# Sequence stage of a fused state-space and expert layer: chunk states in 32-row strips, scores in 32x64 tiles, and paced scatters

## The chip, the cores and the metric

One core of one Trainium2 chip runs the kernel. The metric is the device time in microseconds, as the median of several executions. Everything is float32, except 0/1 tables in bfloat16 for the routing. A float32 product shows as two matmul records and two weight loads in the trace, a float32 transpose and a bfloat16 product as one each.

## The reference

The input x has 2048 tokens of 128 values. The first part is a chunked state-space layer with 16 heads of 8 values, 16 states per head and chunks of 64 tokens:

```python
proj = x @ W_in.T                       # xp | z | B (16x16) | C (16x16) | dt_low (16)
dt = softplus(dt_low @ dt_W.T + dt_b);  dA = dt * -exp(A_log);  dAcs = cumsum(dA) in each chunk
scores = einsum('bcihn,bcjhn->bcijh', Cc, Bc) * exp(dAcs_i - dAcs_j) * causal * dtc
y_intra = einsum('bcijh,bcjhp->bcihp', scores, xc)
chunk_state = einsum('bckhn,bckhp->bchnp', Bc, (dtc * decay_to_end)[..., None] * xc)
h = chunk_decay * h + chunk_state       # one step for each of the chunks, in order
y_cross = einsum('bcthn,bchnp,bcth->bcthp', Cc, h_states, exp(dAcs))
y = (y_intra + y_cross) + xp * D_param
y = y / rms(y) * norm_w * silu(z);      out = y @ W_out.T
x = layernorm(x + out)
```

The second part sends each token to 4 of 16 experts, by the four largest of the logits `-|x - key_e|^2 + x @ rw.T + rb`, with a softmax over the four; an expert is 128 to 512, gelu, 512 to 128. The result is `layernorm(x + the weighted sum of four)`.

## The kernel before

**Stages.** The tokens are 16 tiles of 128 (two chunks each), two tiles to a pair, 8 pairs. A start-up loads the inputs and computes all step sizes and decays. A sequence loop of seven steps (s = 1 to 7) then runs the tiles 2s and 2s + 1 through projection, scores and states, and the older pairs through output, norm and routing. Then come the experts: 64 full and 8 mixed blocks of 128 rows, in four-deep rings, and a final sum and norm. Every engine has its own in-order list of work; semaphores alone tie them together. The order of each list is written out by hand: for TensorE at lines 705 to 729, DVE at 1234 to 1290, ACT at 1731 to 1747, GpSimd at 1868 to 1913. SyncE (SP) issues loads in the order of lines 407 to 420, and the experts' row loads from line 423 on.

**The sequence step on TensorE.** `project` (L530) makes x and B of one tile in rows of tokens, 384 columns. `project_cb` (L539) makes B and C turned, four 128-column products. `scores` (L553) multiplies B with a block-diagonal copy of C (`block_diag`, ACT, L1641, four copies a tile, each masked for one of four heads), in tiles of 64 rows by 64 columns of the array, 256 columns each, into banks 3 and 4. `states` (L563) makes the two chunk states as full 128x128 products, of which only the blocks on the diagonal are of use. DVE carries the state from chunk to chunk by a sum and a scale for each (L949, L958), and `y_cross` (L578) reads it. `y_intra` (L591) uses 16-column tiles; its result, turned, is copied by ACT (`yiT_copy`, L1653) and added to y by `y_back` (L601). `skip_products` (L616), `y_transpose` (L622), `out_product` (L630), `x2_transpose` (L636), `router` (L642) and `positions` (L651 to 655) belong to older pairs and write two banks by turns (`late`).

**DVE and ACT.** DVE masks the scores (`causal`, L965), scales x (`take_x`, L940), forms y (`y_scale`, `y_add`, L990, L998), gates it (`gated`, L1005), adds x (`residual`, L1013), normalizes (`normed`, L1038), and finds the four experts, the slots (`slots`) and the gates. ACT copies between PSUM and SBUF and takes exponentials and logarithms.

**Scatters.** When a pair's normed rows, ids, gates and slots are there, GpSimd sends them to the experts' row table in HBM with eight indirect DMAs (L1860), one for each tile and choice. SP loads the first expert's rows (L447) only when the 40 scatters of pairs 0 to 4 have landed (`EARLY` = 5) and the early table is made. The scatters of pairs 5 and 6 stand in GpSimd's list ahead of the experts' first store of results (L1881), those of pair 7 are mixed with stores 7 to 14.

## Time and profile before

| what | us |
|---|---|
| median of 3 runs | 314.29 |
| lowest and highest run | 314.27, 315.08 |
| span of the profiled execution | 314.5 |
| TensorE busy | 283.4 (90%) |
| DVE busy | 204.3 (65%) |
| ACT busy | 209.2 (67%) |
| GpSimd busy | 143.7 (46%) |

The profiled execution's own time is its span, 314.5 us, from the first to the last instruction on the core; no other time of it is given. The start-up takes up to about 29 us, the sequence loop and its tail up to about 126, the experts up to about 282, the rest is the final sum. In a timeline row stand the start, the time to the end of the last of the merged instructions, the engine, the line, the output and input, and the count; a matmul's end is modelled, so the distance to the next group's start is the better price.

### The profile page before, as it was taken

How to read it: one execution, taken by the hardware profiler on the slowest of the kernel's cores; microseconds unless marked ns; L12 is line 12 of the kernel's file. 1: busy time of each engine (PE TensorE's matmuls, PEld its weight loads, DVE VectorE, ACT ScalarE, POOL GpSimd, SP SyncE). 2: the span in 40 equal slices, each digit the busy share in tenths (PEclk: the TensorE clock that was granted, in tenths of full speed). 3: DMA queues.
4: the chain of work that ended last, by engine and by line, in shares of the span. 5: the costliest groups of instructions: out<-in, count | busy, mean ns of one | idle time of the engine just before them, and what ended most of it. 6: DMA issues, size and time to landing. Idle time of an engine off the chain costs nothing.

```text
span 314.5 us, 10587 instructions
## 1 busy us (share of the span) xinstructions
PE 283.4 (90%) x2948; PEld 250.6 (80%) x2949; DVE 204.3 (65%) x914; ACT 209.2 (67%) x725; POOL 143.7 (46%) x146
## 2 busy tenths in 40 slices
PE   2999899999999997899889899999999999997591
PEld 2986668687677775799779899999999999995480
DVE  2237768898888888866888566555655566641272
ACT  1475466575574743577667688888888889885064
POOL 1200000657456474777677775555555564424000
PEclk9979999999999999599999999999999999999697
DMA  6999920111111111342122232222222222100884
GB/s 212 300 336 374 415 95 2 40 39 57 38 58 48 39 58 47 87 103 78 48 83 90 80 92 72 65 81 71 67 69 67 70 68 60 42 12 6 305 273 92
DMA packets 25260, 33.30 MB, mean 106 GB/s; under 512 B 4299, under 2 KB 18020, under 8 KB 24832
## 3 DMA queue, kind: packets, MB, share of 16 engines
q1 hardware_dynamic: 20432, 23.30, 24.7%
q0 software_dynamic: 4352, 8.79, 7.9%
q10 hardware_dynamic: 432, 0.67, 0.7%
q8 instruction: 22, 0.36, 0.5%
q14 instruction: 22, 0.18, 0.2%
HBM read 21.76 MB, written 11.50 MB: 106 GB/s over the span
## 4 chain that ended last, share of the span: by engine, by line
PE 70%; DVE 11%; DMA 6%; issue 5%; ACT 5%; POOL 1%; DVEq 1%; POOLq 0%; ACTq 0%; SPq 0%
PE bank L774 16%; PE bank L752 15%; PE bank L747 4%; PE bank L539 4%; PE bank L553 4%; DMA yrows<-shared,idi 3%; PE bank L844 3%; PE bank L764 3%; PE bank L530 2%; PE bank L736 2%; PE bank L514 2%; PE bank L591 2%; DMA small<-in_small 2%; PE bank L601 2%; PE bank L563 2%
## 5 line engine op out<-in xcount | busy, mean ns | idle before, releaser
L1881 POOL DMA_INDIRECT yrows<-shared,idi x72 | 75.9, 1054 | 56.1 <-ACT shared L1790 32.6
L1860 POOL DMA_INDIRECT xrows<-rows_all,sli x64 | 62.4, 975 | 81.6 <-issue 63.4
L1769 ACT ACTIVATE shared<-bank,shared 128x128 f32<-128x128 f32 x256 | 73.2, 370 | 19.1 <-PE bank L752 19.1
L752 PE MATMUL bank<-shared 128*128 128x128 f32 x512 | 70.0, 281 | 2.5 <-issue 2.5
L774 PE MATMUL bank<-w2s,shared 128*128 x512 | 68.1, 276 | 0.8 <-DVE shared L1464 0.4
L752 PEld LDWEIGHTS bank<-shared 128*128 128x128 f32 x512 | 63.8, 196 | 3.9 <-issue 3.8
L774 PEld LDWEIGHTS bank<-w2s,shared 128*128 128x128 f32 x512 | 62.3, 192 | 1.4 <-issue 1.4
L1450 DVE COPY shared<-w1s 128x644 f32 x64 | 33.1, 517 | 28.5 <-issue 27.7
L1790 ACT ACTIVATE shared<-shared,idg 128x128 f32<-128x128 f32 x72 | 29.9, 418 | 7.1 <-DVE shared L1464 5.8
L1641 ACT ACTIVATE shared<-bank,small 128x256 f32<-128x256 f32 x64 | 25.1, 476 | 4.7 <-PE bank L539 4.7
L965 DVE TENSOR_TENSOR shared<-bank,small 128x512 f32<-128x512 f32 x32 | 21.2, 682 | 1.3 <-PE bank L553 1.3
L1754 ACT ACTIVATE shared<-bank 128x128 f32<-128x128 f32 x72 | 20.8, 289 | 0.7 <-PE bank L736 0.7
L736 PE MATMUL bank<-cst,shared 128*128 128x128 f32 x72 | 20.5, 284 | 0.0
L1464 DVE TENSOR_TENSOR shared<-bank,shared 128x128 f32<-128x128 f32 x64 | 18.3, 286 | 2.2 <-PE bank L774 1.5
L539 PEld LDWEIGHTS bank<-xT_all,winT 128*128 128x128 f32 x128 | 16.9, 200 | 3.1 <-issue 0.5
L553 PE MATMUL bank<-shared 64*64 64x256 f32 x256 | 18.2, 402 | 0.5 <-issue 0.3
L539 PE MATMUL bank<-xT_all,winT 128*128 128x128 f32 x128 | 18.6, 290 | 0.0
L1429 DVE TENSOR_REDUCE idg<-sel 128x2 f32<-128x8 f32 x72 | 11.6, 161 | 9.6 <-ACT shared L1790 6.7
L1765 ACT ACTIVATE shared<-bank,shared 128x64 f32<-128x64 f32 x64 | 14.0, 329 | 2.4 <-PE bank L747 2.1
L747 PEld LDWEIGHTS bank<-shared 128*128 128x128 f32 x128 | 15.2, 194 | 0.2 <-issue 0.2
L747 PE MATMUL bank<-shared 128*128 128x64 f32 x128 | 15.3, 272 | 0.0
L1422 DVE SCALAR_TENSOR_TENSOR sel<-shared,tb 128x8 f32<-128x8 f32 x64 | 14.0, 219 | 1.8 <-issue 1.7
(221 smaller groups left out, 472.0 us busy)
## 6 DMA issues: line engine op xcount, KB each, us to landing
shared<-xrows SPq DMA_DIRECT2D x64, 70.0 KB
w1s<-in_w1T SPq DMA_DIRECT2D x1, 4128.0 KB, 24.5
w2s<-in_w2T SPq DMA_DIRECT2D x1, 4096.0 KB, 22.9
w1s<-yrows SPq DMA_DIRECT2D x8, 512.0 KB, 7.9
yrows<-shared,idi POOLq DMA_INDIRECT x72
xrows<-zrow SPq DMA_DIRECT2D x1, 1120.0 KB, 13.9
xp_all<-in_xp SPq DMA_DIRECT2D x1, 1024.0 KB, 7.8
w1s<-in_b SPq DMA_DIRECT2D x1, 1024.0 KB, 20.9
```

What stands on the lines that cost most here:

```text
L539: m = mm(bank[2][:, k * P:(k + 1) * P], winT[:, c0:c0 + P], xT_all[:, t * P:(t + 1) * P], start=True, stop=True)
L553: m = mm(bank[3 + r][q * Q:(q + 1) * Q, j * 256:(j + 1) * 256], c_[half, 2 + j, q * Q:(q + 1) * Q], cbd[t % 2][half, j, q, :], start=True, ...
L736: pe.transpose(turned_rows(), xb[b.slot(RB)][:, 0:D], ident).then_inc(s3["bt_mm"], 1)
L747: m = mm(hidden_bank(u)[:, f * P + h * HB:f * P + (h + 1) * HB], wh[:, f * P:(f + 1) * P], xbT[u][:, h * HB:(h + 1) * HB], start=True, sto ...
L752: m = mm(hidden_bank(u)[:, f * P:(f + 1) * P], w[:, f * P:(f + 1) * P], xbT[u][:, :], start=True, stop=True)
L774: m = mm(out_bank(u), hT[u][:, f * P:(f + 1) * P], w2s[:, bass.ds(ex, 1), f, :], start=(f == 0), stop=(f == FB - 1))
L1450: ve.tensor_copy(w1c[r][:], w1s[:, bass.ds(expert_of(mybir.EngineType.DVE, b), 1), :].rearrange("p o f -> p (o f)")).then_inc(s3["w1_dve"], 1)
L1641: m = act(cbd[t % 2][:, :, :, h * Q:(h + 1) * Q], bank[2][:, 0:2 * P].rearrange("p (j q i) -> p j q i", j=2, q=NC), cp, scale=sm("head4")[ ...
L1769: m = act(hT[u][:, f * P:(f + 1) * P], hidden_bank(u)[:, f * P:(f + 1) * P], ACT.Gelu, bias=w[:, F + f:F + f + 1])
L1790: act(yw[r][:], yb[u][:], cp, scale=idg[r][:, 1:2]).then_inc(s3["yw_act"], 1)
L1860: po.indirect_dma_start(out=xrows, out_offset=bass.IndirectOffsetOnAxis(ap=sli[:, g, k:k + 1], axis=0), in_=rows_all[:, g, :], in_offset=N ...
L1881: po.indirect_dma_start(out=yrows, out_offset=bass.IndirectOffsetOnAxis(ap=idi[r][:, 0:1], axis=0), in_=yw[r][:, :], in_offset=None, bound ...
```

## The change

It rewrites the sequence stage and the lists of all engines around it.

- Scores: the masks are for two heads (`head2`), `block_diag` makes two copies a tile, and the products are tiles of 32 rows by 64 columns with 128 columns each, 16 a tile, into four banks (3, 4, 6, 7).
- States: eight products of 32 columns for each tile, which make only strips of use (`states_at`, in bank 7). DVE forms the four new states of a pair in one product (`new_states`) and carries them by one scan over 160 values (`carry`). Four ACT copies of 32 rows each (`states_out`) spread them into zeroed tiles `hs`. GpSimd prepares the factors (`chunk_factors`). `scores` and `states` wait for `ds_dve`, since they share bank 7.
- `project` makes x only; B in rows of tokens comes from two transposes of ACT's copy `cb`.
- `y_cross` and `y_back` run once a pair, with the two halves of the columns by turns; `skip_products` go to bank 5.
- `out_product` adds x itself through the identity, and carries 16 more columns for the logits (`idkw`, `woutn`, width 144). `residual`, `x2_transpose`, `x2_copy` and `router` go; `xp_all` (1 MB) is not loaded; W_out in its other order and the identity are.
- The normed rows of pairs 0 to 5 and the packing of ids move from DVE to ACT (`rows_normed`, `ids_packed`); the gates' sum comes from ACT's accumulator. There is one bank for the outputs (`late`), not two.
- `positions` multiplies the one-hot tables themselves, 20 products; counts are kept as running bases (`next_base`); the products for counts go.
- Scatters of pairs 0 to 4 wait, two at a time, for points in TensorE's list (`paced`).

The core of the diff:

```diff
+            def paced(m_, i):
+                s = m_ + 3
+                if i == 0:
+                    po.wait_ge(s1["sc_mm"], 2 * s)
+                if i == 2:
+                    po.wait_ge(s1["yt_mm"], s - 1)
+                if i == 4:
+                    po.wait_ge(s1["y_mm"], s)
+                if i == 6:
+                    po.wait_ge(s1["sc_mm"], 2 * s + 2)
...
             def project(t):
                 after(s1["b_act"], t)
+                pe.wait_ge(s1["cb_act"], t + 1)
+                mm(bank[0][:, 0:D], xT_all[:, t * P:(t + 1) * P], winT[:, 0:D], start=True, stop=True)
+                for j in range(2):
+                    m = pe.transpose(bank[0][:, (j + 1) * P:(j + 2) * P], cb[t % 4][:, 2 + j, :], ident)
...
             def scores(t):
+                after(s1["ds_dve"], (t + 1) // 2)
-                        for r in range(2):
-                            half = slice(r * Q, (r + 1) * Q)
-                            m = mm(bank[3 + r][q * Q:(q + 1) * Q, j * 256:(j + 1) * 256], c_[half, 2 + j, q * Q:(q + 1) * Q],
-                                   cbd[t % 2][half, j, q, :], start=True, stop=True, skip_group_check=True)
+                        for r, b in enumerate(score_banks):
+                            rows = slice(r * HR * NS, (r + 1) * HR * NS)
+                            m = mm(bank[b][q * Q:(q + 1) * Q, j * P:(j + 1) * P], c_[rows, 2 + j, q * Q:(q + 1) * Q],
+                                   cbd[t % 2][rows, j, q, :], start=True, stop=True, skip_group_check=True)
...
             def states(t):
+                for g in range(2 * H // 4):
+                    j, r = divmod(g, 4)
+                    to = states_at[r * HR * NS:(r + 1) * HR * NS, j * Q:(j + 1) * Q].rearrange("p (a s x) -> p a s x", a=2, s=2)
+                    m = mm(to[:, :, t % 2, :], bs[t % 2][:, g * 32:(g + 1) * 32],
+                           xz[t % 4][:, g * 32:(g + 1) * 32].rearrange("p (a x) -> p a x", a=2), start=True, stop=True, skip_group_check=True)
...
+            def y_cross(m_):
+                pe.wait_ge(s1["e_act"], m_ + 1)
+                pe.wait_ge(s1["cb_act"], 2 * m_ + 2)
+                pe.wait_ge(s1["yit_act"], 2 * m_ + 2)
...
+            def y_intra(t):
+                if t % 2:
+                    pe.wait_ge(s1["yit_act"], t)
+                else:
+                    after(s1["y_dve"], t // 2)
...
+            def states_out(m_):
+                ac.wait_ge(s1["h_dve"], m_ + 1)
+                after(s1["yc_mm"], m_ - 1)
+                for r in range(4):
+                    rows = slice(r * HR * NS, (r + 1) * HR * NS)
+                    m = act(hs[m_ % 2][rows, :, :, r * 2 * HD:(r + 1) * 2 * HD],
+                            chunk_states(m_)[rows, :, :, 0:CP].rearrange("p (j a) w c -> p c j (a w)", j=2), cp)
...
+            def new_states(m_):
+                ve.wait_ge(s1["st_mm"], 2 * m_ + 2)
+                tt(chunk_states(m_)[:, :, :, 1:CP + 1].rearrange("p a w c -> p a c w"),
+                   states_at.rearrange("p (a c w) -> p a c w", a=4, c=CP),
+                   gmx[:, m_, :].rearrange("p (a w c) -> p a c w", a=4, w=HD)[:, :, 1:CP + 1, :], ALU.mult).then_inc(s1["ds_dve"], 1)
+            def carry(m_):
+                at_m = hx[:, CP * m_:CP * m_ + 4 * HD * (CP + 1)]
+                ve.tensor_tensor_scan(at_m, gmx[:, m_, :], at_m, 0.0, ALU.mult, ALU.add).then_inc(s1["h_dve"], 1)
...
             for s in range(1, NP):                       # TensorE's list
+                tile(scores, 2 * s - 2, first=2)
+                pair(y_cross, s - 2, first=0)
+                pair(skip_products, s - 2, first=0)
+                pair(y_back, s - 2, first=0)
+                tile(project_cb, 2 * s, first=4)
+                tile(states, 2 * s - 1, first=3)
+                tile(y_intra, 2 * s - 2)
+                pair(positions, s - 3)
+                tile(scores, 2 * s - 1)
+                tile(project, 2 * s, first=2)
+                pair(y_transpose, s - 2)
+                tile(project_cb, 2 * s + 1, first=3)
+                pair(out_product, s - 2)
+                tile(project, 2 * s + 1, first=3)
+                tile(states, 2 * s, first=2)
+                tile(y_intra, 2 * s - 1)
...
             for s in range(1, NP):                       # DVE's list
+                pair(new_states, s - 1, first=1)
+                pair(place, s - 3)
+                pair(gated, s - 2)
+                tile(causal1, 2 * s - 1)
+                tile(take_x, 2 * s, first=2)
+                pair(gates, s - 3)
+                tile(causal0, 2 * s - 1)
+                pair(carry, s - 1, first=1)
+                pair(res_stats, s - 2)
+                pair(res_moments, s - 2)
+                pair(slots, s - 3)
+                tile(take_x, 2 * s + 1, first=3)
+                pair(square_sums, s - 2)
+                pair(neg_means, s - 2)
+                pair(key_bias, s - 2)
+                pair(logits, s - 2)
+                tile(causal1, 2 * s)
+                tile(causal0, 2 * s)
+                pair(best, s - 2)
+                pair(y_scale, s - 1)
+                pair(below_best, s - 2)
+                pair(y_add, s - 1)
+                pair(best_ids, s - 2)
+                pair(one_hot, s - 2)
...
             for s in range(1, NP):                       # ACT's list, conditions at its end left out
+                tile(yiT_copy, 2 * s - 1)
+                pair(rows_normed, s - 2)
+                tile(block_diag, 2 * s + 1)
+                pair(ids_packed, s - 3, first=0)
+                tile(take_b, 2 * s + 1, first=3)
+                pair(gate_exp, s - 2)
+                    pair(square, s - 1, first=0)
+                tile(cb_copy, 2 * s + 2, first=4)
+                    pair(log_ms, s - 1, first=0)
+                    pair(inv_rms, s - 1, first=0)
+                tile(block_diag, 2 * s + 2, first=4)
+                    pair(yT_copy, s - 1, first=0)
+                    tile(yiT_copy, 2 * s, first=2)
+                tile(take_b, 2 * s + 2, first=4)
+                tile(cb_copy, 2 * s + 3, first=5)
+                    pair(states_out, s, first=1)
+                    pair(log_var, s - 1, first=0)
+                    pair(inv_dev, s - 1, first=0)
...
             scores(14); y_cross(6); skip_products(6); y_back(6); y_intra(14); states(15); scores(15)   # TensorE's tail,
             early_blocks(); positions(5); y_transpose(6); y_intra(15); out_product(6)                 # one call a line
             y_cross(7); skip_products(7); y_back(7)                                                   # in the file
```

## Rows read from the trace of the kernel before

**Rows 1.** Windows: stretch, each engine's busy time and (instructions), PEclk, DMA share, GB/s.
```profile
37.05:49.90 12.85, 12.40 (x176) 9.41 (x176) 8.85 (x31) 7.95 (x25) 0.00 (x0) 1.00 0.32 133
...
88.18:101.04 12.86, 12.27 (x179) 9.26 (x178) 10.97 (x50) 7.80 (x25) 7.68 (x9) 1.00 0.14 46
...
182.00:246.00 64.00, 64.00 (x576) 64.00 (x575) 38.46 (x174) 54.16 (x204) 36.33 (x35) 1.00 0.25 73
```

**Rows 2.** TensorE's timeline, loop start and one step: start, us, engine, line, names, records.
```profile
29.47 0.81 PE L530 MATMUL bank<-winT,xT_all 128*128 128x384 f32 x2
...
79.09 1.05 PE L539 MATMUL bank<-xT_all,winT 128*128 128x128 f32 x8
80.08 1.09 PE L553 MATMUL bank<-shared 64*64 64x256 f32 x16
81.10 0.44 PE L622 MATMUL bank<-cst,yg 128*128 128x128 f32 x2
81.47 0.97 PE L578 MATMUL bank<-hs,shared 128*64 128x64 f32 x16
82.36 0.71 PE L630 MATMUL bank<-woutn,yT 128*128 128x128 f32 x4
83.01 0.64 PE L591 MATMUL bank<-shared,xz 128*16 128x64 f32 x32
83.58 1.09 PE L553 MATMUL bank<-shared 64*64 64x256 f32 x16
...
86.08 0.44 PE L636 MATMUL bank<-cst,rows_all 128*128 128x128 f32 x2 [0.57 <-DVE rows_all L1038]
86.36 0.61 PE L563 MATMUL bank<-xz,bs 128*128 128x128 f32 x4
86.99 0.62 PE L642 MATMUL bank<-kw,x2T 128*128 128x16 f32 x4
87.54 0.64 PE L591 MATMUL bank<-shared,xz 128*16 128x64 f32 x32
...
89.65 0.97 PE L601 MATMUL bank<-cst,yiT 128*64 128x64 f32 x16
90.54 0.71 PE L616 MATMUL bank<-wxd,xTp 128*128 128x128 f32 x4
91.09 0.17 PE L652 MATMUL bank<-msk,before 128*128 128x16 bf16 x1
...
91.22 0.89 PE L530 MATMUL bank<-winT,xT_all 128*128 128x384 f32 x2
91.95 1.05 PE L539 MATMUL bank<-xT_all,winT 128*128 128x128 f32 x8
```

**Rows 3.** Timeline of all engines, start of the experts.
```profile
124.32 32.61 SPq L447 DMA_DIRECT2D shared<-xrows  x16
...
126.75 0.42 PE L736 MATMUL bank<-cst,shared 128*128 128x128 f32 x1
```

**Rows 4.** Groups by line, two steps (75.35 to 101.04): names, shapes, count, busy, mean ns.
```profile
L949 DVE TENSOR_TENSOR st<-hs,bank 128x128 f32<-128x128 f32 x8 | 2.2, 281 | 1.3 <-PE bank L563 1.3
L958 DVE TENSOR_TENSOR hs<-st,gm 128x128 f32<-128x128 f32 x8 | 2.2, 272 | 0.0
...
L1641 ACT ACTIVATE shared<-bank,small 128x256 f32<-128x256 f32 x16 | 6.3, 475 | 1.3 <-PE bank L539 1.3
```

**Rows 5.** Timeline of all engines, one hand-over from TensorE to ACT.
```profile
88.25 0.38 ACT L1653 ACTIVATE yiT<-bank 128x256 f32<-128x256 f32 x1 [1.04 <-PE bank L591]
```

**Rows 6.** GpSimd's timeline, last scatters of pair 6 and the first store.
```profile
139.25 0.96 POOL L1860 DMA_INDIRECT xrows<-rows_all,sli  x1 [0.30 <-issue]
140.52 0.96 POOL L1860 DMA_INDIRECT xrows<-rows_all,sli  x1 [0.30 <-issue]
...
142.52 1.04 POOL L1881 DMA_INDIRECT yrows<-shared,idi  x1 [0.19 <-issue]
```

**Rows 7.** DMA issues by line: kind, count, median us from issue to landing.
```profile
xrows<-rows_all,sli POOLq DMA_INDIRECT x64, 2.3
```

728 lines of the change are left out of this document (342 added, 386 removed).

## The prediction

> **What bounds the kernel now.** I read the busy time by stretches first, then TensorE's own timeline of one step, then DVE's and ACT's groups, GpSimd's timeline, and last the start of the experts. From 37 to 114 us the steps of the sequence loop repeat: TensorE is busy 12.4 and 12.3 of 12.85 us, DVE 11.0 of 12.86, ACT 7.8, GpSimd 7.7, at full clock [rows 1]. In one whole step, 79.09 to 91.95 = 12.86 us, one product group starts where the one before ends, but for one hole: x2_transpose (L636) comes 0.57 us late behind DVE's normed rows [rows 2]. So TensorE's queue is the bound and a step costs what its products cost. The stretch without scatters (37.05 on) takes as long as the one with eight of them [rows 1]: scatters cost the products nothing here. The experts, 182 to 246, have TensorE busy 64.00 of 64 us [rows 1]; the change leaves their products alone, so what it is worth is how much earlier they begin. Their first transpose runs at 126.75, 2.43 us after SP issued the first load of rows at 124.32 [rows 3].
>
> **TensorE's step, part by part.** A price is the distance between two starts in [rows 2].
> - Scores: a group of eight 64x64-tile products of 256 columns takes 80.08 to 81.10, 1.02. Eight in a row, at the 0.25 of a 128-column product (L539: four in 0.99) doubled, would take 4.0, so about four run at once. The new group has 16 products of 128 columns in 32x64 tiles, eight places: half the column work. They are 32 records, and the narrowest group here, L591, issues 32 records in 0.57 (83.01 to 83.58, 18 ns each). I take 0.60; bounds 0.57 and, if the tiles queued, 16 x 0.25 = 4.0. Two per step: 2.04 becomes 1.20.
> - y_cross and y_back: 0.89 each for eight (81.47 to 82.36, 89.65 to 90.54), every run of them in one half of the columns. Now the two halves alternate, as L591 alternates four column tiles. I take 0.5 each; bounds 0.45 and 0.89.
> - States: 0.63 for two full products (86.36 to 86.99); now eight of 32 columns, 16 records at 18 ns = 0.29. I take 0.3 each; bounds 0.29 and 0.63. 1.26 becomes 0.6.
> - project: 384 columns, 0.73 (91.22 to 91.95); now one 128-column product (0.25) and two transposes of cb, a transpose being 0.37 / 2 (L622) at most. I take 0.45 each; bounds 0.25 + 0.2 and the old 0.73. 1.5 becomes 0.9.
> - x2_transpose (86.08 to 86.36, 0.28), its hole (0.57), router (86.99 to 87.54, 0.55) go: 1.4 off. out_product was 0.65 for two (82.36 to 83.01); now four, 144 columns wide: 4 x 0.25 x 144 / 128 = 1.1, 0.4 on.
> - positions: five bf16 products in 0.13 (91.09 to 91.22) become 20: 0.52, 0.4 on.
> - Unchanged: project_cb 2 x 1.0, y_intra 2 x 0.57, skip products 0.55, y_transpose 0.3.
> Sum after: 1.2 + 0.5 + 0.5 + 0.6 + 0.9 + 1.1 + 0.5 + 2.0 + 1.1 + 0.55 + 0.3 = 9.3 us for 12.86.
>
> **A rule on narrow products.** The 32 records of L591 come 18 ns apart [rows 2], with four tiles taking turns. The Trainium skill, TensorEngine Tiling (Array Packing), section Performance Considerations, has every matmul carry about 60 cycles of overhead, so that one column costs as much as sixty; at 2.4 GHz that is 25 ns. The five bf16 products of positions, which share no tiles, come 26 ns apart [rows 2], as the page says; L591 undercuts it, so the overhead overlaps between tiles and I keep 18 ns. Without that overlap the sum would be 1.3 us a step longer (rival 2 has its price from the rows).
>
> **What then ends last.** DVE loses the four sums and four scales of a step (0.28 each, 2.2 in all [rows 4]) and gets one product of 128 columns (0.28) and one scan of 160 (0.35 at the same rate), loses the residual, the normed rows and the id copies: 11.0 falls to about 7.5. ACT loses four of its eight block_diag copies (6.3 us for 16 of them, 0.39 each [rows 4]: 1.6), and x2_copy, and gains four copies of 32 rows (states_out), two normed rows, a second exponential, ids and the sums of gate_exp: 7.8 - 2.0 + about 2.8 = 8.6. Neither is over 9.3, but both queues now stand in a ring with TensorE. I walked one step: y_intra of the even tile waits for y_add, which waits for y_back; project_cb waits for ACT's block_diag, which is queued behind the normed rows, and these wait for DVE's logits; y_transpose waits for gated behind inv_rms; y_cross waits for yiT_copy, which is queued on ACT behind states_out, log_var and inv_dev. A hand-over costs 0.14 to 0.2 us (y_intra's 32 records from 87.54 on take till 88.11, the copy of them starts at 88.25 [rows 2, 5]). With the groups' durations I get holes of 0.5 at project_cb, 0.3 at y_transpose and 0.1 at y_cross. I take 0.9 in all; bounds 0 (everything covered) and 2.2 (these holes more than doubled). Step: 9.3 + 0.9 = 10.2.
>
> **GpSimd.** Scatters start 1.27 us apart when nothing holds them (139.25, 140.52), so eight take 10.1 [rows 6]. That is more than 9.3: GpSimd is nearly a bound of its own. A new pace holds pair m's eight, two at a time, to scores, y_transpose, y_back and scores of steps m+3 and m+4; the last two of pair 4 wait for scores(15). They are on the path: SP loads the first rows only after all 40 scatters of pairs 0 to 4 have landed. Behind the waiting scatters are only scatters and, later, the experts' stores; GpSimd's added chunk_factors run before the loop; no row prices them. The first gates new_states(0), which DVE's table work delays anyway: I take nothing, with a store's 1.3 as the upper end.
>
> **The sum.** The loop starts near 29.47 [rows 2]; two extra loads, a key product ahead of dt_products and kT's load put before winT's cost about as much (0 to 1.5) as the thinner start-up gives back (0.6). Step 1 has 3.9 us of products; it waits for tables, states_out and copies; between 3.9 and a full step I take 7.6. Step 2: 9.5, the logits of a pair being not yet there. Steps 3 to 7: 5 x 10.2 = 51.0. To the end of scores(15): 5.7. Then the second of two scatters starts 1.6 later (0.3 + 1.27), lands 2.3 after that [rows 7], SP's wait and read of the row address take 0.9 (bounds 0.3, GpSimd's own gap, and 2.4, the load itself), the load 2.4 [rows 3]: 7.2. 29.5 + 7.6 + 9.5 + 51.0 + 5.7 + 7.2 = 110.5. TensorE's rest of the tail (positions, y_transpose, y_intra, out_product, y_cross, skip, y_back and their waits, some 6) fits beside these 7.2. The experts start 126.75 - 110.5 = 16.2 us earlier.
> Is it kept? The first store (L1881) ran at 142.52, 15.8 after the first transpose, right behind the 16 scatters of pairs 5 and 6 [rows 6]. After: 18 x 1.27 + 1.2 = 24.0 from scores(15), 16.8 after the first transpose: 1 us worse. The count product with its wait in the middle of the experts goes: about 1 us better. Net 0, bounds -1.5 and +1.5. Span 314.5 - 16.2 = 298.3; the median of the runs (314.29) lies 0.2 under the span: **298**.
>
> **Rivals.**
> 1. GpSimd alone bounds. If the holes close (step 9.3 to 9.7), pair 0 goes at 29.5 + 7.6 + 9.5 + 6.0 = 52.6, the 40th scatter starts 0.3 + 39 x 1.27 = 49.8 later, 102.4, and the experts begin at 108.0: 295.8. For: 10.1 is above 9.3. Against: the rings through ACT. Chance 0.17.
> 2. The rings cost double, or narrow products don't overlap their fixed cost. Double: step 11.1, six steps 5.4 us more, 303.4. The 160 narrow records of a step (64 scores, 32 states, 64 y_intra) at the 26 ns of positions in place of 18: 1.3 more a step, 7.8 in the time, 306. With both 311. (By that rule of the Trainium skill the second half would hold.) For: ACT's 8.6 in a fixed order, one output bank in place of two. Chance 0.2.
> 3. The experts' start doesn't carry the gain: stores and scatters on GpSimd are back to back after 142.52, and if they, not TensorE, set the time to 182, a gain in the loop only lengthens the queue. For: 16 scatters, 20 us, stand ahead of the first store. Against: they start with scores(15), so they move too. If two thirds or more stayed behind: 309 to 314. Chance 0.06.
> 4. Slower: the eight 32x64 tiles don't run at once. No row shows quarter-row tiles. At 16 x 0.25 = 4.0 a group the step is 9.3 + 2 x 3.4 = 16.1 and the time 298 + 6 x 5.9 = 333. It decides once a step passes 12.9. Against: four column tiles (L591) and 2x2 tiles (L553) do overlap. Chance 0.05.
> A scan at half the rate of an ordinary DVE operation is what the Trainium skill has (DVE: opcode table, instruction layouts, handler registers and perf-mode slots, section Datapath and trigger behaviour); no row has a scan of this size. By it carry takes 0.5, not 0.35, ahead of states_out: 1 us in the time.
>
> **Chances and range.** Forecast 0.52 (own range 295.5 to 302). With rivals 1 and 2 it spans 293 to 306, which holds about 8 in 10; low end is rival 1 with a better start of the experts, high end rival 2. A change under 0.3% (0.9 us) can't be told from none. Faster 0.92, same 0.02 (top of rival 3), slower 0.06.
>
> **What would show it.** Steps of 10.2; score groups of 0.6; y_cross and y_back about 0.5; TensorE idle ahead of project_cb and y_transpose; scatters of pair 4 ending two behind scores(15); first transpose near 110.5. Wrong if score groups stay at 1.0 or more, if a step passes 11.2, or if the experts' start moves by 16 and the end does not.

## The result and the profile after

The changed kernel takes 314.15 us (median of 20 runs, 309.52 to 317.07) beside 315.41 us (20 runs, 314.22 to 317.43) of the kernel before on the same chip: ratio 0.9884, 95% interval 0.9856 to 0.9911. The ratio leaves out runs more than 1.5% above the fastest one of their kernel, 10 of the changed kernel's 20 and none of the other's, so it flatters the change: over all runs the medians stand at 0.996 and the means (313.62 and 315.55) at 0.994. The changed kernel is faster, by 0.4 to 1.2% as one counts, where 5% were forecast; 298 us with a range of 293 to 306 was wrong. The execution shown here took 313.46 us, with a span of 311.6; the traces compared below are 2.9 us apart in their spans (314.5 and 311.6), more than the medians.

Windows of the changed kernel, in answer to [rows 1]: step 3, step 7 and the experts' steady part.

```profile
51.20:61.67 10.47, 9.61 (x257) 8.35 (x251) 8.06 (x34) 8.51 (x31) 0.00 (x0) 1.00 0.02 3
93.44:104.10 10.66, 9.71 (x257) 8.44 (x251) 8.79 (x40) 8.33 (x31) 7.58 (x8) 1.00 0.18 58
182.00:246.00 64.00, 64.00 (x576) 64.00 (x576) 38.12 (x169) 54.16 (x204) 35.83 (x34) 1.00 0.25 71
```

A step fell from 12.86 us to between 10.5 and 10.7 (10.2 forecast). TensorE's timeline of one step, in answer to [rows 2]:

```profile
82.87 0.70 PE L576 MATMUL bank<-shared 32*64 32x128 f32 x32
84.24 0.69 PE L603 MATMUL bank<-hs,shared 128*64 128x64 f32 x16 [0.67 <-ACT yiT L1596]
84.86 0.71 PE L641 MATMUL bank<-wxd,xTp 128*128 128x128 f32 x4
85.50 0.69 PE L632 MATMUL bank<-cst,yiT 128*64 128x64 f32 x16
86.46 1.13 PE L561 MATMUL bank<-xT_all,winT 128*128 128x128 f32 x8 [0.28 <-issue]
87.52 0.33 PE L589 MATMUL bank<-xz,bs 128*32 128x32 f32 x16
87.67 0.63 PE L622 MATMUL bank<-shared,xz 128*16 128x64 f32 x32
88.23 0.36 PE L675 MATMUL bank<-oh,before 128*128 128x16 bf16 x8
...
88.83 0.69 PE L576 MATMUL bank<-shared 32*64 32x128 f32 x32
89.45 0.49 PE L548 MATMUL bank<-winT,xT_all 128*128 128x128 f32 x2
...
91.10 0.41 PE L661 MATMUL bank<-idkw,xTp 128*128 128x144 f32 x2
...
92.13 0.46 PE L548 MATMUL bank<-winT,xT_all 128*128 128x128 f32 x2
```

The distance from start to start gives the prices: a score group (L576) 88.83 to 89.45, 0.62; y_cross (L603) 0.62; states (L589) 0.15; y_intra (L622) 0.56; positions 88.23 to 88.83, 0.60; out_product (L661 and its partner) 91.10 to 92.13, 1.03.

The first transpose of the experts came at 123.14 us, against 126.75 [rows 3] and the 110.5 forecast. Four rows of the timeline show what it waited for: the slots of pair 0 on DVE (L1092), its expert numbers on ACT (L1643), the first and the 40th scatter on GpSimd (POOL).

```profile
61.50 0.28 DVE L1092 TENSOR_REDUCE sli<-ohs 128x8 int32<-128x128 f32 x1
...
65.04 0.22 ACT L1643 ACTIVATE rows_all<-i 128x8 f32<-128x8 uint32 x1
...
66.26 1.18 POOL L1826 DMA_INDIRECT xrows<-rows_all,sli  x1 [28.43 <-ACT rows_all L1643]
...
117.68 0.96 POOL L1826 DMA_INDIRECT xrows<-rows_all,sli  x1 [0.30 <-issue]
```

TensorE's rows with a wait, from 104 us on:

```profile
105.86 0.69 PE L603 MATMUL bank<-hs,shared 128*64 128x64 f32 x16 [1.07 <-ACT yiT L1596]
108.89 0.64 PE L622 MATMUL bank<-shared,xz 128*16 128x64 f32 x32 [1.08 <-DVE yr L983]
111.01 0.70 PE L576 MATMUL bank<-shared 32*64 32x128 f32 x32 [1.32 <-DVE hx L949]
115.17 0.69 PE L652 MATMUL bank<-cst,yg 128*128 128x128 f32 x2 [2.62 <-DVE yg L990]
123.14 0.30 PE L745 MATMUL bank<-cst,shared 128*128 128x128 f32 x1 [1.75 <-DMA shared<-xrows]
```

So two chains end close together: TensorE's tail at 121.4, and the rows at 123.14. SP issued the first load of rows at 121.12, 3.44 us behind the start of the 40th scatter, and the early table had long been there (115.3). In the kernel before, the 40th scatter started at 117.01 and the load waited for the early table (123.3): the steps became shorter, but the 40th scatter did not come sooner.

The last transpose stands at 276.25 (278.0 before), so of 3.6 us at the first transpose 1.75 are left. Between the two, TensorE has two holes that the kernel before has not (its longest ones there are 1.29, 0.67 and 0.62). Rows of DVE's and TensorE's timelines:

```profile
139.79 0.16 DVE L1023 TENSOR_TENSOR rw<-rv 128x2 f32<-128x2 f32 x1 [1.97 <-POOL rv L1894]
...
142.27 0.50 DVE L1383 COPY shared<-w1s 128x644 f32 x1 [0.36 <-issue]
142.87 1.13 PE L760 MATMUL bank<-shared 128*128 128x128 f32 x8 [1.48 <-issue]
...
171.11 0.50 DVE L1383 COPY shared<-w1s 128x644 f32 x1 [0.84 <-issue]
171.71 2.04 PE L760 MATMUL bank<-shared 128*128 128x128 f32 x8 [2.54 <-issue]
```

Both times TensorE goes on right behind DVE's copy of the expert's weights. The first copy comes late behind pair 7's root (`rv`), a small operation that stands in GpSimd's list behind the 16 scatters of pairs 5 and 6; the second stands behind DVE's run of table instructions (167.57 to 169.8). That these two are the causes is read from the rows; no run removed them.

### The profile page after: what moved, and what is told of

Its sections match the earlier page's. It is cut to its first block, busy times and chain, and to the rows that moved or that the text cites. A ratio compares the mean times of both kernels' runs of the same rounds, so it can differ in the third digit from the quotient of the medians.

```text
span 311.6 us, 11662 instructions
## 1 busy us (share of the span) xinstructions
PE 271.9 (87%) x3534; PEld 252.2 (81%) x3535; DVE 186.0 (60%) x817; ACT 215.2 (69%) x763; POOL 152.2 (49%) x167
## 3 DMA queue, kind: packets, MB, share of 16 engines
q0 software_dynamic: 4352, 8.79, 8.2%
## 4 chain that ended last, share of the span: by engine, by line
PE 74%; ACT 6%; DVE 6%; issue 6%; DMA 5%; SPq 1%; POOL 0%; ACTq 0%; POOLq 0%; DVEq 0%
PE bank L760 20%; PE bank L781 19%; PE bank L755 5%; PE bank L561 4%; PE bank L745 3%; ACT hs L1570 3%; PE bank L842 3%; PE bank L771 3%; PE bank L532 2%; PE bank L576 2%; PE bank L603 2%; DVE shared L962 2%; PE bank L641 1%; DMA small<-in_small 1%; PE bank L499 1%
## 5 line engine op out<-in xcount | busy, mean ns | idle before, releaser
L1888 POOL DMA_INDIRECT yrows<-shared,idi x72 | 76.7, 1065 | 57.3 <-ACT shared L1752 31.4
L1733 ACT ACTIVATE shared<-bank,shared 128x128 f32<-128x128 f32 x256 | 73.2, 369 | 20.1 <-PE bank L760 20.1
L760 PEld LDWEIGHTS bank<-shared 128*128 128x128 f32 x512 | 64.8, 198 | 6.1 <-issue 6.1
L781 PE MATMUL bank<-w2s,shared 128*128 x512 | 69.0, 279 | 0.2 <-DVE shared L1396 0.2
L781 PEld LDWEIGHTS bank<-w2s,shared 128*128 128x128 f32 x512 | 63.6, 195 | 0.5 <-issue 0.4
L561 PE MATMUL bank<-xT_all,winT 128*128 128x128 f32 x128 | 19.5, 300 | 1.5 <-issue 1.4
L561 PEld LDWEIGHTS bank<-xT_all,winT 128*128 128x128 f32 x128 | 17.5, 212 | 2.7 <-issue 2.6
L1364 DVE TENSOR_REDUCE idg<-sel 128x2 f32<-128x8 f32 x72 | 11.6, 161 | 11.5 <-ACT shared L1752 8.8
L1570 ACT ACTIVATE hs<-hx 32x128 f32<-32x128 f32 x32 | 13.8, 431 | 3.7 <-DVE hx L956 3.4
L755 PEld LDWEIGHTS bank<-shared 128*128 128x128 f32 x128 | 15.2, 194 | 0.2 <-issue 0.2
L622 PE MATMUL bank<-shared,xz 128*16 128x64 f32 x512 | 11.2, 231 | 2.7 <-DVE woutn L886 1.6
## 6 DMA issues: line engine op xcount, KB each, us to landing
xrows<-zrow SPq DMA_DIRECT2D x1, 1120.0 KB, 11.6
```

The source lines that it names most:

```text
L561: m = mm(bank[2][:, k * P:(k + 1) * P], winT[:, c0:c0 + P], xT_all[:, t * P:(t + 1) * P], start=True, stop=True)
L755: m = mm(hidden_bank(u)[:, f * P + h * HB:f * P + (h + 1) * HB], wh[:, f * P:(f + 1) * P], xbT[u][:, h * HB:(h + 1) * HB], start=True, sto ...
L760: m = mm(hidden_bank(u)[:, f * P:(f + 1) * P], w[:, f * P:(f + 1) * P], xbT[u][:, :], start=True, stop=True)
L781: m = mm(out_bank(u), hT[u][:, f * P:(f + 1) * P], w2s[:, bass.ds(ex, 1), f, :], start=(f == 0), stop=(f == FB - 1))
L1570: m = act(hs[m_ % 2][rows, :, :, r * 2 * HD:(r + 1) * 2 * HD], chunk_states(m_)[rows, :, :, 0:CP].rearrange("p (j a) w c -> p c j (a w)", ...
L1733: m = act(hT[u][:, f * P:(f + 1) * P], hidden_bank(u)[:, f * P:(f + 1) * P], ACT.Gelu, bias=w[:, F + f:F + f + 1])
```

## Where 12.6 us went

| stretch | forecast | measured | more |
|---|---|---|---|
| to the start of step 2 | 37.1 | 41.47 (of it 3.8 before the loop's first product could start, 33.25 for 29.47) | 4.4 |
| step 2 | 9.5 | 9.73 | 0.2 |
| steps 3 to 7 | 51.0 | 52.9 (51.20 to 104.10) | 1.9 |
| to the end of scores(15) | 5.7 | 7.5 (waits of 1.07, 1.08, 1.32) | 1.8 |
| from there to the first transpose | 7.2 | 11.5 (TensorE's own tail 9.8, the rows 1.7 behind it) | 4.3 |

## The experiments

Five sittings, each with the kernel before beside it. The chips were of two sorts, which had not been expected; each of the five had another chip, so a chip and the time of its sitting are not told apart. On the first sort the kernel before takes 315.5 us (the result above and the second sitting). On the second sort (four chips, the other four sittings) it takes 388.5 to 389.9, and the changed kernel 379.34. All kernels lose most of it while the scatters run, told below; what a wait costs on the first sort can be read on the second only up to the first scatter. Medians, and ratios to the kernel before with their 95% intervals:

| kernel | first sort | second sort |
|---|---|---|
| changed | 314.15, 313.81; 0.9884 [0.9856, 0.9911], 0.9929 [0.9902, 0.9957] | 379.34; 0.9748 [0.9686, 0.9811] |
| no holds | 314.97; 0.9832 [0.9796, 0.9867] | 390.47; 0.9976 [0.992, 1.0032] |
| numbers early | | 367.16; 0.9461 [0.9407, 0.9515] |
| tail order | | 377.3; 0.9702 [0.9651, 0.9753] |
| numbers and tail | 312.2; 0.9893 [0.9864, 0.9923] | 365.51; 0.9411 [0.9358, 0.9464] |
| start-up | 311.61; 0.9853 [0.9819, 0.9887] | |
| strips split | | 375.1, 373.81, 373.74; 0.9651 [0.9621, 0.9681], 0.9619 [0.9553, 0.9684], 0.9589 [0.9542, 0.9637] |
| table order | | 378.17; 0.9731 [0.9699, 0.9763] |
| all four | | 363.55, 362.34, 366.26; 0.9353 [0.9322, 0.9383], 0.9269 [0.9182, 0.9356], 0.9392 [0.9338, 0.9445] |
| all and tables | | 364.87; 0.934 [0.9245, 0.9434] |

On the first sort the changed kernel's own runs spread over 9 us, and a median and its ratio can point different ways ("no holds" has the higher median and the lower ratio); differences under 1% between two kernels are read from the traces.

**The control**, twice.

> The changed kernel itself, as the control of the four runs before, in which engines stood still with no releaser (the row says issue) while scatters ran, and the kernel before took 388.5 us. Theory S (on such a chip scatters hold up the engines' supply of instructions, and the holds of the change limit that): this kernel takes 372 to 378 us there, 12 us or more less than without the holds, and a step of the sequence stage takes about 20 us from the first scatter on. Theory N (the stillness comes from the edits): 314 us there too. On a chip without the stillness: 314 us, steps of 10.6.

> The changed kernel, as the control of the three runs beside it. On a chip without the stillness 313 to 314 us, steps of 10.6, the first transpose 19.05 us behind the start of step 8. On one with it 376 to 379 us, as with the tables' order alone (378.2), against 388 to 389 for the kernel before.

313.81 and 379.34 us: the slowness of the second sort belongs to the chip or the sitting, not to the edits. On the first sort the first transpose stood 19.06 us behind the start of step 8 (19.04 in the first trace).

**No holds.** 

```diff
                 for i in range(2 * TOPK):
-                    if m_ < NP - 3:
-                        paced(m_, i)
                     send_one(m_, i)
```

> The four waits that hold GpSimd's scatters of pairs 0 to 4 in front of chosen products are left out; nothing else changes. In the changed kernel the first scatter goes at 66.26 us, the 40th at 117.68, and the waits hold it back by 1.8 us in all. Theory (two bounds stand close together before the experts: the scatters' chain, first transpose at 123.14, and TensorE's own tail, which ends at 121.4): the 40th scatter goes at 115.9, the first expert's transpose at 121.4 to 121.9, the time falls by 1.2 to 1.8 us against the changed kernel (about 312.7). Rival (the holds pay, because scatters beside the narrow products slow them): the steps of the sequence stage, 10.6 us now, grow to 10.8 or more, the 40th scatter gains nothing and the time rises by 1 us or more. Third: no step and no time moves by more than 0.3 us, then the chain of scatters isn't what the experts wait for.

> The holds left out, once more, beside the changed kernel on the same chip. Where the engines stand still during scatters: 385 to 392 us, 12 us or more above the changed kernel. On a chip without it: theory of the two bounds gives 312.7 (first transpose 121.4 to 121.9, steps 10.6); the rival, that scatters slow narrow products everywhere, gives 315 or more.

On the first sort nothing moved: the 40th scatter starts 51.39 us behind the first with the holds gone (51.42 and 51.45 with them), and the first transpose 19.16 behind the start of step 8. My expected gain of 1.8 us fell: the gaps between pairs are not made by the holds. On the second sort the kernel without the holds stands at 0.9976 of the kernel before, with them at 0.9748, in two sittings: there the holds are worth some 9 us, nearly all that the whole change brings.

**Numbers early**, alone and with **tail order**. The first line stands in the middle of ACT's step, the second edit at its end, the last lines in ACT's tail.

```diff
-                pair(ids_packed, s - 3, first=0)
...
                     pair(inv_dev, s - 1, first=0)
+                pair(ids_packed, s - 2, first=0)
...
-            ids_packed(5)
-            states_out(7)
             square(6)
             log_ms(6)
             inv_rms(6)
+            states_out(7)
```

> ScalarE's copy of the expert numbers of a pair stands at the end of the step in which VectorE finds them, not in the middle of the next. Theory: it is this copy that releases the first scatter, so that goes at 61.8 us (end of the slots of pair 0) and not at 66.26; from there readiness sets the pace, one pair a step of 10.6, and the 40th goes at about 113 and not at 117.68. The experts' first transpose then has TensorE's own tail ahead of it (121.4): it comes at 121.4 to 121.9 and not at 118.5, and the time falls by 1.2 to 1.8 us, no more than without the holds. Rival (the experts' start hangs on the scatters alone): first transpose 118.5, time lower by 4 us or more. Rival (the chip's 1.27 us a scatter bounds all): the 40th doesn't move.

> On ScalarE, behind the last step, the root mean square of pair 6 (square, log, exp) stands ahead of the copy of pair 7's states, not behind it. In the changed kernel the transpose of pair 6's gated rows waits 2.62 us for it, and TensorE runs at half clock in the 4 us behind that hole. Theory: this wait falls to about 1.3 us, TensorE's tail ends at 118.5 to 120 and not at 121.4, and the experts' first transpose stays at 123.1, since the scatters' chain is the later of the two: the time stays within 0.5 us. Rival (the tail is what sets the start): the first transpose comes 1.4 us or more earlier and the time falls by as much.

> The two edits together: expert numbers copied in their own step, and the root mean square of pair 6 ahead of the states of pair 7. Theory (two bounds, each hiding the other): the 40th scatter goes at about 113, TensorE's tail ends at 118.5 to 120, and the first transpose comes at 119 to 120, 3 to 4 us earlier than in the changed kernel; the time falls by 3 to 4 us (about 310.5), more than the sum of the two alone (1.5 + 0). Rival (the clock or the tables set the experts' start): no more than 1.5 us.

> Expert numbers in their own step and the root mean square of pair 6 ahead of pair 7's states, beside the changed kernel on the same chip. Theory of the two bounds: 3 to 4 us less than the changed kernel on a chip without the stillness (first transpose at 119 to 120). Where the engines stand still during scatters: 365 us, some 8 us or more below the changed kernel, because earlier scatters leave fewer to the tail. Rival: no more than 1.5 us in either case.

On the first sort, both edits together, step 3 started at 52.51. GpSimd's first scatter stands 12.52 us behind that, not 15.06; the 40th 11.21 behind the start of step 8 (105.37), not 13.58. TensorE's rows of that trace:

```profile
115.50 0.69 PE L652 MATMUL bank<-cst,yg 128*128 128x128 f32 x2 [0.96 <-DVE yg L990]
...
122.09 0.30 PE L745 MATMUL bank<-cst,shared 128*128 128x128 f32 x1 [0.66 <-DMA shared<-xrows]
```

The first transpose comes 16.72 behind the start of step 8, 2.3 us sooner. So readiness is what releases the scatters, and ACT's copy of the numbers was one part of it, though a smaller one (2.5 us) than the 4.4 us I gave it: put at the end of ACT's step it runs at 63.83, still 0.75 behind the slots, since it now stands behind the roots of the next pair, and in both traces the first scatter starts another 1.0 us behind the end of that copy. In all five traces of this kind of chip the first transpose comes 5.4 to 5.5 us behind the start of the 40th scatter. The median fell by 1.6 us (313.81 to 312.2), within the spread of the control's runs. That two bounds hide each other was not shown: neither edit ran alone on the first sort. On the second sort, numbers early alone makes 0.9461 of the kernel before, tail order alone 0.9702, which is no clear gain over 0.9748.

**Start-up order.** TensorE's key product (L541, L543) and states(1) ahead of decays(2) (the counts that the key product waits for are changed with it); on DVE and ACT:

```diff
             row_constants(0)
-            chunk_sums(2)
-            input_factors(2)
             router_bias(0)
             out_keys(0)
             new_states(0)
             carry(0)
+            chunk_sums(2)
+            input_factors(2)
...
-            states_out(0)
             block_diag(2)
+            states_out(0)
```

> Start-up reordered: TensorE makes the router's key products ahead of the last decays, VectorE takes them up and makes the first states before the last chunk sums, ScalarE's block-diagonal copy of tile 2 stands ahead of the first states' copy. The products within the chunks of tile 0 then don't wait 1.62 us for the router's weights. Theory (the sequence stage starts late because of this wait and what follows it): step 2 starts at about 39.9 and not at 41.5, every later step and the experts' start 1.6 us earlier, the time falls by 1 to 1.6 us. Rival (TensorE's clock falls in another place instead, the start is a matter of its clock): step 2 within 0.5 us of 41.5.

The wait of 1.62 us before y_intra(0) went, and another came, for `cb_copy(3)`, which stands on ACT behind states_out(0), with half clock behind it. TensorE's rows of its timeline:

```profile
33.49 1.13 PE L561 MATMUL bank<-xT_all,winT 128*128 128x128 f32 x8 [0.80 <-issue]
36.34 0.77 PE L548 MATMUL bank<-winT,xT_all 128*128 128x128 f32 x2 [1.72 <-ACT shared L1578]
```

The windows of that stretch, columns as in [rows 1]:

```profile
34.00:38.00 4.00, 2.28 (x39) 1.79 (x41) 0.70 (x2) 2.15 (x6) 1.99 (x5) 0.70 0.93 391
38.00:42.00 4.00, 4.00 (x84) 3.13 (x74) 1.35 (x3) 1.50 (x4) 0.00 (x0) 0.50 0.36 152
```

Step 2 starts at 38.69, but lasts 11.23 and not 9.73: step 3 starts at 49.92 (51.20 and 51.99 in the controls; 49.82 without the holds and 52.51 with numbers and tail, which touch nothing here). Within that scatter the one trace shows no sure gain; the median is 2.2 us under the control.

**The kernel before, once more** (second sort), and TensorE's clock in the start-up.

> The kernel before, once more, for its trace on this chip. If TensorE's half clock in the start-up belongs to the changed kernel's order, the granted clock of 20 to 34 us is near full here, as in the first trace (1.00 in 24 to 28), and the loop's first products come at 29.5; if it is a matter of chance, they come up to 3 us later. On a chip on which scatters hold up the engines it shows holes without a releaser in its own sequence stage.

One execution, 382.57 us. The sequence stage of the kernel before stands still here too: from its first to its 40th scatter pass 92.9 us, against 60.1 on the first sort. Windows of this trace of the kernel before:

```profile
19.60:28.00 8.40, 8.40 (x64) 6.16 (x64) 6.01 (x21) 5.26 (x16) 0.00 (x0) 0.80 1.06 393
28.00:38.00 10.00, 8.72 (x144) 6.18 (x145) 8.09 (x29) 3.93 (x12) 0.00 (x0) 1.00 1.05 390
```

Of the changed kernel, first trace:

```profile
19.60:28.00 8.40, 7.35 (x84) 6.51 (x85) 3.63 (x12) 3.89 (x11) 1.23 (x4) 0.59 1.07 381
28.00:38.00 10.00, 8.38 (x122) 7.27 (x121) 5.82 (x20) 4.92 (x15) 5.77 (x13) 0.67 1.04 409
```

Of one of the traces with all four edits (below), the one with the fullest clock:

```profile
19.60:28.00 8.40, 6.13 (x104) 5.36 (x103) 5.71 (x21) 3.98 (x12) 2.49 (x8) 0.88 1.06 377
28.00:38.00 10.00, 8.19 (x213) 6.70 (x213) 6.29 (x16) 4.88 (x14) 4.58 (x10) 1.00 1.03 400
```

The kernel before shows the same granted clock in both of its traces: 0.80, then 1.00. In both kernels TensorE falls to the lower level (1.2 GHz) near 20 us, behind a stretch without idle time (16 to 20 in the first trace of each: busy 4.00 of 4.00 us at 1.00); the kernel before is back by 24 us (24 to 28: 1.00), the changed one, with 1.05 us idle at states(0) (it waits for ACT's `take_b`) and 1.62 at y_intra(0), is not for long: over 28 to 38 its start-up order has 0.61 to 0.83 in 13 traces, the kernel before 1.00 in two, the version with all four edits 0.83, 0.84, 1.00 and 1.00. So the lower level in 28 to 38 goes with the changed kernel's start-up; how much of it there is differs from trace to trace of one order, and no run moved the clock alone.

**Strips split.** Two of the four copies of `states_out` (the loop in the first two lines, on ACT) go to DVE, right behind the scan; `y_cross` waits for both.

```diff
-                for r in range(4):
+                for r in range(2):
...
+            def strips_out(m_):
...
+                ve.wait_ge(s1["h_dve"], m_ + 1)
+                after(s1["yc_mm"], m_ - 1)
+                for r in range(2, 4):
+                    rows = slice(r * HR * NS, (r + 1) * HR * NS)
+                    m = ve.tensor_copy(hs[m_ % 2][rows, :, :, r * 2 * HD:(r + 1) * 2 * HD],
+                                       chunk_states(m_)[rows, :, :, 0:CP].rearrange("p (j a) w c -> p c j (a w)", j=2))
+                m.then_inc(s1["e_dve"], 1)
```

> Of the four strips in which pair m's states go from the scan's tile to the tile that TensorE reads (four copies on ScalarE, 1.75 us a step), two are copied by VectorE right behind the scan; nothing else changes. Theory (ScalarE's row of work, 8.5 us and more of a step of 10.6, ends the wait of 0.6 us before the products with the states): the wait is gone, a step takes 9.9 to 10.1 us and not 10.6, step 8 starts 3 us earlier measured from step 3, the first transpose 3 us earlier, the time falls by 2 to 3 us against the changed kernel on the same chip. Rival (VectorE, 8 us a step, takes the place of ScalarE): 10.4 or more a step. Rival (the scatters' cadence of 1.27 us, 10.1 for eight, bounds behind it): steps 10.0, but the first transpose gains less than 1.5.

> Two of the four strips of states copied by VectorE, on a chip where the steps can be read. In the last run, before its scatters began, step 3 took 9.92 us against 10.46 in the changed kernel. Theory (ScalarE's strips end the wait before the products with the states): steps 3 to 7 take 9.9 to 10.1 us each and not 10.5 to 10.7, step 8 and the first transpose come 2.7 us earlier, the time falls by 2 to 2.7 us against the control. Rival (VectorE or the scatters' cadence binds from the scatters on): steps of 10.3 or more, or a first transpose that gains less than 1.5.

> Half of the strips of states on VectorE. On a chip without the stillness: steps of 9.9 to 10.1 us and not 10.6, the first transpose 2.7 us earlier than in the changed kernel, the time 2 to 2.7 us below it, near 311.5; by the rival (VectorE or the scatters' cadence binds) 10.3 or more a step or 313 us. On a chip with it: 372 to 376 us, 5 us below the changed kernel.

Three times on the second sort. Step 3, the last without scatters, takes 9.92, 9.90 and 9.91 us and not 10.46: ScalarE's strips did end the wait, and DVE did not take its place. In step 4, before the first scatter, the wait at y_cross is 0.28 or 0.29 us, for 0.67. So five steps give 0.55 + 4 x 0.38 = 2.1 us, an estimate; no run on the first sort has it. With steps of 10.2 us GpSimd's eight scatters (8 x 1.27 = 10.1) would stand right behind as the next bound. On the second sort the edit gives 5.5 us (379.34 to 373.81, same sitting).

**All four edits** (numbers early, tail order with `gated(6)` ahead of `causal1(15)`, strips split, start-up order with `cb_copy(3)` ahead of `states_out(0)`).

> Four edits together: expert numbers in their own step; pair 6's root mean square ahead of pair 7's states and its gating ahead of tile 15's masks; half of the strips on VectorE; the start-up order, with the copy of tile 3's products ahead of the first states' copy. Theory (the missed gain is the sum of separate small waits): step 2 starts at 39 to 40, steps of 9.9 to 10.1, step 8 at 99, the 40th scatter at 111 (39 times 1.265 behind a first one at 61.7), the first transpose at 116.5, 6 to 7 us earlier than in the changed kernel; the time falls by 5 to 6 us, to 308. Rival (something else holds the experts' stage, so that an earlier start is given back): first transpose as said, but the time no more than 2 us lower.

> The four edits together (numbers in their own step, root mean square of pair 6 and its gating early, split strips, start-up order with tile 3's copy ahead of the first states). Theory (sum of separate waits): steps of 9.9 to 10.1, step 8 at 98 to 99.5, the first transpose 16 us or less behind it, at 114.5 to 116.5, and the time 5 to 6 us below the control, about 308. Rival (the experts' stage gives the earlier start back: it already lasted 0.5 to 1.7 us longer where it began earlier): the first transpose as said, the time no more than 3 us below.

> The four edits together. On a chip without the stillness: steps 3 to 7 of 9.9 to 10.1 us, step 8 at 98 to 99.5, the first transpose at 114.5 to 116.5 by the sum of separate waits and the time near 308, a ratio of 0.976 to 0.98 to the kernel before; by the rival, that the experts' stage gives the earlier start back, the time is 311 or more. On a chip with it: 358 to 365 us once more, 0.93 of the kernel before.

Step 3 starts at 48.13, 45.72 and 46.54 us (47.49 with the table order on top) and lasts 9.91. In the ten traces that have neither the new start-up order nor the split it starts at 47.10 to 52.59, 51.0 on average; with the strips alone at 47.92, 49.33 and 49.39. So the four edits give back about 4 us of the start-up, the split some 2 of them, and the ranges overlap. The time is 362.34 beside 379.34 for the changed kernel and 389.85 for the kernel before: this version beats both on the second sort. Whether it reaches 308 on the first is open: the last sittings met no such chip.

**Table order**, alone and on top of the four: `rows_of` and `row_table` ahead of block 17, the other three behind blocks 17, 18 and 19.

```diff
-            moe(17)
             rows_of()
             row_table()
+            moe(17)
             valid()
+            moe(18)
             penalties()
+            moe(19)
             halves()
...
```

> In the experts' stage VectorE makes the late blocks' tables in one run of 15 small instructions behind block 17; there TensorE stands 2.54 us (171.71, no releaser shown) and then runs at half clock to 175. Here the first two functions go ahead of block 17 and the other three behind blocks 17, 18 and 19. Theory (the copy of the next expert's weights stands behind the run): the hole shrinks below 1 us, the last transpose stands 151.5 us behind the first and not 153.1, the time falls by 1 to 1.6 us. Rival (the experts' stage is bound by TensorE's products or the scatters behind it, a hole is made up): 0 to 0.3 us.

> The same with the late blocks' tables spread on VectorE (two functions ahead of block 17, three behind blocks 17, 18, 19). Theory (VectorE's run of 15 small instructions makes TensorE's 2.5 us hole at 171.7 and the half clock behind it): no hole above 1 us there, the experts' stage 1 to 1.6 us shorter than with the four edits alone, the time as much lower, about 306.5. Rival: the hole comes from something else, 0 to 0.3 us.

Inconclusive (364.87 beside 362.34 without it). On the second sort the control has a hole of 2.52 us beside the tables (234.04), but holes of 2.69 and 2.66 us stand in the traces with the new order too, where the run of table instructions is broken up, and all three end with ACT's gelu (L1733 in the control): they are not the hole of 171.71, which no run on the first sort took away.

## What happens on the second sort

The changed kernel's control there. Steps without scatters take 10.46 us as on the first sort, steps with them 18.6 to 20.2. GpSimd's timeline over one such step:

```profile
95.92 0.95 POOL L1826 DMA_INDIRECT xrows<-rows_all,sli  x1 [2.86 <-PE bank L576]
97.18 0.96 POOL L1826 DMA_INDIRECT xrows<-rows_all,sli  x1 [0.30 <-issue]
105.73 0.96 POOL L1826 DMA_INDIRECT xrows<-rows_all,sli  x1 [7.59 <-ACT rows_all L1643]
...
112.04 0.96 POOL L1826 DMA_INDIRECT xrows<-rows_all,sli  x1 [0.30 <-issue]
```

TensorE's timeline over the same step:

```profile
96.97 1.91 PE L561 MATMUL bank<-xT_all,winT 128*128 128x128 f32 x8
98.68 0.69 PE L661 MATMUL bank<-idkw,xTp 128*128 128x144 f32 x2
...
107.75 0.27 PE L622 MATMUL bank<-shared,xz 128*16 128x64 f32 x3 [0.43 <-issue]
108.45 0.30 PE L622 MATMUL bank<-shared,xz 128*16 128x64 f32 x3 [0.44 <-issue]
...
111.37 0.22 PE L678 MATMUL bank<-oh,ones 128*128 128x16 bf16 x2 [1.16 <-issue]
...
114.23 0.19 PE L681 MATMUL bank<-oh,ones 128*128 128x16 bf16 x1 [1.15 <-issue]
```

Two scatters in front of 128-column products (95.92, 97.18) leave no hole, though the products run at the lower clock (0.50 from 94.4 to 100.6). Six in a run (105.73 to 113.0), in front of narrow products, leave TensorE one to four records at a time, with nothing in between that the profile shows as a wait. From 106.17 to 114.35 pass 8.2 us for what takes 1.15 on the first sort (98.24 to 99.39), so 7.0 are lost there, and another 1.5 at the lower clock up to the next step (114.35 to 120.57 for 99.39 to 104.10). Other engines stand as well, beside pair 5's eight scatters of 160.68 to 170.49. ACT's and DVE's timeline of the same trace:

```profile
172.13 0.28 ACT L1719 ACTIVATE shared<-bank 128x128 f32<-128x128 f32 x1 [8.08 <-remote]
...
172.16 0.42 DVE L976 TENSOR_TENSOR yr<-bank,fC 128x256 f32<-128x256 f32 x1 [7.63 <-remote]
```

ACT's copy waits for a transpose that ended at 164.7, DVE's operation for products that ended at 164.5; both go on 1.6 us after the last scatter ended, within 0.03 us of each other. A hold of TensorE, ACT and DVE while scatters run, starting once they have used up some work that they already had, fits: the wide products L561 are 8 records in 1 us, the narrow L622 are 32 in 0.56. That the supply of instructions is what stands behind the scatters is an inference from this pattern; no run took the supply apart. It fits the order of the second column. A step with eight scatters takes 22.1 us on average without the holds (11.6 more than one without scatters), 19.7 with them (9.2 more), 17.9 with the numbers early (7.4 more; there the run starts 1.7 us into the step and not 3.8), and 17.0 to 17.3 with all four edits (7.1 to 7.4 more than 9.9). The holds are meant to spread the scatters, but in the control six of eight still run in one go, because the row at 105.73 shows them released by the late numbers (7.59 us idle, ended by ACT L1643), when the points in TensorE's list are long past.

## Why the prediction was wrong, step by step

- **The bound, TensorE's queue.** Right. The prices: score group 0.60 forecast, 0.62 measured; y_cross and y_back 0.5, 0.62 and 0.61 (43.40 to 44.01, where no hole follows); states 0.3, 0.15; the two `project` 0.9, 1.15 (100.02 to 100.56, 102.69 to 103.30); out_product 1.1, 1.03; positions 0.52, 0.60. "I walked one step" gave 0.9 us of holes, and there are 0.9 to 1.0, though two thirds are at y_cross, given 0.1. Step 10.2, measured 10.47 to 10.68. Rival 4 (tiles not at once, 333) is refuted by the first row of L576, rival 2's double rings by the steps, its 26 ns a narrow record by 19, 9 and 18 ns.
- **ACT, "7.8 - 2.0 + about 2.8 = 8.6".** The sum held (8.33 to 8.51). Inside it, states_out takes 1.75 us, and it is that one that makes most of the 0.6 at y_cross; the split shows it. DVE was put at 7.5 and has 8.06 to 8.79, without harm to the steps.
- **"Step 1 ... between 3.9 and a full step I take 7.6", and a loop start "near 29.47".** This failed, and is the largest term: 4.4 us, 3.8 of them before the loop. I took the old start for the new one and set the added start-up work against what the thinner products give back. The new order leaves TensorE idle for 1.05 us and then 1.62, and its clock stays at the lower level for much of 20 to 38, which its thinner products can't make up. How the 3.8 divide between order and clock is open: one order alone lets step 3 begin anywhere from 47.10 to 52.59, all four edits from 45.72 to 48.13.
- **"A new pace holds pair m's eight".** This failed. I took the holds for what releases a scatter, and rival 1 put pair 0 at 52.6. It goes at 66.26, released by the pair's readiness: slots at the end of step 3, 61.50, and numbers, put by the change into the middle of ACT's next step, 65.04. From there the 40 scatters need 51.4 us whatever the holds: four steps of 10.6 and one pair's own 8.9 (7 x 1.27). So the 40th starts 6.0 us behind the end of scores(15) (111.64), where I had 1.6. The rest of that chain was right: 5.5 us to the first transpose, 5.6 forecast. The section on the kernel before names the four things a scatter needs (normed rows, ids, gates and slots); I never gave them their times in the new order.
- **"TensorE's rest of the tail ... some 6 ... fits beside these 7.2".** Failed: it took 9.8 (111.64 to 121.4), with 2.62 idle behind gated(6), whose root stood on ACT behind states_out(7), and half clock behind it (0.50 from 115.17 to 119). Alone it would have put the first transpose 2.6 us later than forecast; the scatters add only 1.7 to that. Ahead of it, step 8's three waits (1.07, 1.08, 1.32) make the 1.8 of "to the end of scores(15): 5.7", for which the prediction gives no waits of their own.
- **"Is it kept? ... Net 0".** This failed by 1.9 us, outside its bounds of 1.5: 3.6 us at the first transpose are 1.75 at the last. The first store came 16.8 behind the first transpose, as forecast; what I left out are the two holes shown above. The experts' stage lasted 153.1 to 154.8 us in five traces of the first sort against 151.3 before, and all five have both: 1.48 to 2.75 us near 142, behind a root that DVE awaits from GpSimd for 1.97 to 3.24 us (0.86 in the kernel before), and 1.95 to 2.54 near 171.5, with a granted clock of 0.79 to 0.84 from 168 to 176 (1.00 before). The first is rival 3's mechanism on a small scale, GpSimd's queue of scatters behind an earlier start. What each is worth is open.
- **"Scatters cost the products nothing here".** Right on that chip, wrong on four others.
- The Trainium skill, DVE: opcode table, instruction layouts, handler registers and perf-mode slots, section Datapath and trigger behaviour, has the scan at half the rate. The trace agrees: carry (160 values) takes 0.48 to 0.49 us, the 0.5 that half the rate gave and not the 0.35 of the sum.
- The Trainium skill, TensorEngine Tiling (Array Packing), section Performance Considerations, has every matmul carry about 60 cycles of overhead. The trace differs for tiles that take turns: 16 records of states follow in 0.15 us, 9 ns each, and 32 of a score group in 0.62, 19 ns each, so what each costs by itself overlaps, as I had assumed.

## What to carry to other kernels

Give every condition of a released step its own time, in the new order of each engine; a wait that is added is a bound only if it is the last of them. A stage that gets shorter brings its start-up and its tail with it: these were 10.5 of the 12.6 us missed, much of it in holes over 1 us, some with TensorE at its lower clock behind them. Ask the same of small operations on an engine with a long queue: 16 scatters stood ahead of one root. Time a change that moves indirect DMAs on more than one chip.

## What the runs showed of the hardware

- Two sorts of chips (or of sittings): the same kernel 315.5 and 389 us. On the second, TensorE, ACT and DVE stand while indirect scatters (1.27 us apart on both) run, up to 8 us at a time.
- There, two scatters in front of wide products leave no hole, six in front of narrow ones cost about 7 us, and the clock is at 0.5 behind them.
- 32x64 tiles do run together: 32 records of a score group take 0.62 us, 19 ns each, beside 124 ns for a record of a full 128-column product (L539, eight in 0.99), so between six and seven at a time.
- 40 scatters are held by their pairs' readiness, one pair a step: 51.4 us with the holds and without them.
- An ACT copy of 32 rows by 128 values with strides takes 0.43 us on average, longer than one of 128 rows and 256 values without (0.36 to 0.39).
